# Causal scores in 64-token blocks with block-diagonal keys, in a gated linear-attention and ternary-FFN layer

## The reference

```python
Q, K, V = x @ Wq.T, x @ Wk.T, x @ Wv.T           # (B, L, H, 16) each
g = sigmoid(x . gw);  log_c = clip(cumsum(log g), -30, 30)
Gc = exp(log_c) + 1e-6;  R = silu(K . sw)
S = cumsum(K V^T * R / Gc, axis=1) * Gc           # a 16 x 16 state for every token
attn = (Q S) @ Wo.T
h = bitlinear(x, w_fc) + gate * (x @ v.T @ fast_b.T @ u.T)
ffn = bitlinear(relu(h) ** 2, w_proj)
out = x + attn + ffn                              # inside attn and ffn, x is normalised
```

## Time and profile before

| | us |
|---|---|
| median of 3 runs | 637.83 (637.13 to 639.09) |
| span of the profiled execution | 637.8 |
| PE busy | 620.1 (97%) |
| PEld busy | 545.8 (86%) |
| DVE busy | 528.7 (83%) |
| ACT busy | 443.3 (70%) |
| POOL busy | 387.3 (61%) |

### The profile page before, as it was taken

One profiled execution on the slowest core, in us unless ns is written; L12 is line 12 of the kernel. 1 busy time (PEld: TensorE's weight loads), 2 busy tenths in 40 slices (PEclk: granted clock), 3 DMA queues, 4 the chain that ended last, 5 costly groups with the idle time before them and its releaser, 6 DMA issues.

```text
span 637.8 us, 21397 instructions
## 1 busy us (share of the span) xinstructions
PE 620.1 (97%) x7710; PEld 545.8 (86%) x7710; DVE 528.7 (83%) x1241; ACT 443.3 (70%) x1036; POOL 387.3 (61%) x505
## 2 busy tenths in 40 slices
PE   7789999999999999999999999999999999999997
PEld 7667888888888888888888888888888888888886
DVE  7678978899888888898789988798988887897863
ACT  4568766677776667776666767775777766677664
POOL 4896666555656665556566565655565665666454
PEclk7689999999999999999999999999999999999999
DMA  9446656886796887866788887668887477775631
GB/s 303 104 97 107 131 106 147 136 145 131 139 147 109 141 138 130 143 133 128 121 145 132 132 146 145 125 106 136 134 143 151 117 137 131 135 130 124 115 54 51
DMA packets 190361, 83.31 MB, mean 131 GB/s; under 512 B 121888, under 2 KB 189728, under 8 KB 190256
## 3 DMA queue, kind: packets, MB, share of 16 engines
q1 hardware_dynamic: 188016, 79.32, 68.4%
q10 hardware_dynamic: 2240, 2.62, 1.3%
HBM read 12.43 MB, written 8.39 MB: 33 GB/s over the span
## 4 chain that ended last, share of the span: by engine, by line
PE 89%; POOL 4%; issue 2%; DMA 2%; SPq 1%; DVE 1%; ACT 1%; ACTq 0%; DVEq 0%; POOLq 0%
PE y_bank L2447 17%; PE attn_bank L2384 9%; PE hid_b L2418 8%; PE hid_a L2418 8%; PE front_b L2313 7%; PE y_bank L2462 7%; PE front_b L2272 7%; PE front_a L2294 6%; PE attn_bank L2397 4%; PE score_a L2346 4%; PE score_b L2346 4%; PE hid_b L2420 2%; PE hid_a L2420 2%; PE score_b L2361 2%; POOL sq_l L821 1%
## 5 line engine op out<-in xcount | busy, mean ns | idle before, releaser
L1871 DVE TENSOR_TENSOR sq_l<-relu_sq,sq_h 128x512 f16<-128x512 f32 x128 | 115.8, 907 | 3.7 <-ACT relu_sq L1162 2.6
L2447 PE MATMUL y_bank<-wproj_t,sq_h 128*128 128x256 f16 x504 | 117.0, 273 | 0.2 <-DVE sq_l L1871 0.2
L2447 PE MATMUL y_bank<-wproj_t,sq_l 128*128 128x256 f16 x504 | 117.0, 273 | 0.0
L1829 DVE TENSOR_TENSOR masked<-score_a,shapes_sb 128x512 f32<-128x512 f32 x128 | 88.2, 689 | 29.6 <-PE score_a L2346 29.0
L1829 DVE TENSOR_TENSOR masked<-score_b,shapes_sb 128x512 f32<-128x512 f32 x128 | 87.5, 684 | 14.0 <-PE score_b L2346 13.7
L746 POOL TENSOR_TENSOR state_diag<-state,state_mask 128x256 f32<-128x256 f32 x56 | 46.8, 836 | 70.7 <-DVE state L1847 34.3
L1153 ACT ACTIVATE sq_h<-relu_sq 128x512 f16<-128x512 f32 x128 | 79.0, 618 | 0.9
L1162 ACT ACTIVATE relu_sq<-relu_sq 128x512 f32<-128x512 f32 x128 | 78.7, 616 | 0.8 <-DVE sq_l L1871 0.7
L2418 PE MATMUL hid_b<-xt,wfc_t 128*128 128x256 f16 x512 | 73.6, 273 | 0.0
L2418 PE MATMUL hid_a<-xt,wfc_t 128*128 128x256 f16 x512 | 73.4, 273 | 0.1
L672 POOL TENSOR_SCALAR xn<-x_sb,neg_mean,rstd 128x256 f32<-128x256 f32 x64 | 42.3, 662 | 50.1 <-DVE rstd L1723 49.9
(11 more groups left out here) (224 smaller groups left out, 1656.9 us busy)
## 6 DMA issues: line engine op xcount, KB each, us to landing
q_diag<-q SPq DMA_DIRECT2D x256, 64.0 KB, 2.8
k_stack<-k SPq DMA_DIRECT2D x128, 128.0 KB, 4.3
x_sb<-in_x SPq DMA_DIRECT2D x32, 256.0 KB, 3.2
out_y<-y_both SPq DMA_DIRECT2D x31, 256.0 KB, 3.2
relu_sq<-in_w_fc ACTq DMA_DIRECT2D x1, 1024.0 KB, 11.5
pj_nat<-in_w_proj ACTq DMA_DIRECT2D x1, 1024.0 KB, 14.2
y_both<-in_w_qk ACTq DMA_DIRECT2D x1, 512.0 KB, 5.1
w_stage<-in_w_qkvz_t SPq DMA_DIRECT2D x1, 512.0 KB, 6.7
```

The lines of the kernel that those rows point to most:

```text
L1829: nc.vector.tensor_tensor(masked[:, c, g].rearrange("p (h n) -> p h n", h=4), score_bank[g % 2][:].rearrange("p (h n) -> p h n", h=4), cau ...
L1871: nc.vector.tensor_tensor(sq_l[:, q], sq[:, n], sq_h[:, q], ALU.subtract).then_inc(sq_l_done, 1)
L2447: last = mm(out_part(b, u, c), part[:, q, at:at + P], wproj_t[:, 2 * q + i], start=(q == i == n == 0 and (c == 0 or last_of_all(b, u))), s ...
```

## The change

- **Scores.** A chunk has `WAVES` = 3 waves. The stationary is now the 64 keys of both heads of a pair side by side (128 columns, block-diagonal in `k_diag`), and the moving operand is `q_stack`, the queries without padding. Waves 0 and 1: 4 matmuls each with the first 64 keys against all 128 queries. Wave 2: 8 matmuls with the later 64 keys against the later 64 queries. The block of later keys against earlier queries, which the mask made zero, is no longer computed.
- **Mask.** 6 a unit instead of 8, each still 512 columns, with a triangle for two heads (`causal_two`).
- **Values.** A chunk still has 16 column-tiled matmuls, but 8 move 128 columns and 8 move 64. The stationary is `v_pair`: rows 0 to 63 one head, rows 64 to 127 the other, so one matmul sums over both heads.
- **v_pair and v_all.** POOL writes the plain product `v_all` (for `state_updates`) in two steps, and in two more (`keep_rows`, 64 partitions x 256) the halves of `v_pair` that stay in their rows; DVE writes the other halves in two steps (`move_rows`, 64 partitions x 256, into the other 64 partitions).
- **DMAs of a unit.** `turn_keys` 2 transposes of 64 partitions instead of 1 of 128; `stack_keys` 8 of 128 KB instead of 4; `stack_queries` 4 of 128 KB instead of 8 of 64 KB.
- **Order.** All slots, prologues and epilogues are written anew. x is loaded and normalised one unit earlier, `queries_t` runs one unit earlier. In the prologue ACT does `fc_sums` ahead of the first `rstd_guess`, POOL `fc_highs(0)` ahead of the first `normalise`.

The diff, cut to its core; the new order of PE's slot is given whole:

```diff
-Q_DMAS, K_DMAS = 2 * PART, PART
+Q_DMAS, K_DMAS = PART, 2 * PART
+SUB = P // 2
+WAVES = 3
+ROW = CH * KT * 2 * P
...
             def stack_queries(b, u):
...
+                for n, part in enumerate((0, 1, 0, 1)):
+                    sp.dma_start(q_stack[32 * n:32 * n + 32, par], q16[:, part]).then_inc(q_stacked[par], 16)
...
             def turn_keys(b, u):
...
+                for h in range(2):
+                    sp.dma_start(k16[:].rearrange("p s (x h) z n -> p (s x) h z n", h=2)[:, :, h, 0],
+                                 k_tok16[SUB * h:SUB * h + SUB].rearrange("p s c d -> p (s c d)"),
+                                 transpose=True).then_inc(k_turned[u % 2], 16)
...
             def stack_keys(b, u):
...
+                for s in range(2):
+                    to = k_diag[:, par, SUB * s:SUB * s + PAIRS // KT * ROW].rearrange("p (g n) -> p g n", n=ROW)
+                    for n, part in enumerate((0, 0, 1, 1)):
+                        sp.dma_start(to[32 * n + HD * s:32 * n + HD * (s + 1)],
+                                     k16[64 * s:64 * s + 64, part]).then_inc(k_stacked[par], 16)
...
+            def keep_rows(b, u):
...
+                for s in range(2):
+                    rows = slice(SUB * s, SUB * s + SUB)
+                    nc.gpsimd.tensor_tensor(block_of(par, rows, s, s), heads_of(vg[:, par, :, 0:D], rows, s),
+                                            weights_of(par, rows, s), ALU.mult).then_inc(v_kept_done, 1)
...
+            def move_rows(b, u, s):
...
+                nc.vector.tensor_tensor(block_of(par, to, s, 1 - s), heads_of(vg[:, par, :, 0:D], rows, 1 - s),
+                                        weights_of(par, rows, 1 - s), ALU.mult).then_inc(v_moved_done, 1)
...
             def scores(b, u, c, g):
...
+                to = score_bank[(WAVES * c + g) % 2]
+                if g < KT:
+                    for i in range(PAIRS // KT):
+                        last = mm(to[:, i * P:(i + 1) * P], keys_of(par, i, c, g, 0),
+                                  q_stack[:, par, KT * i + g, c * P:(c + 1) * P], start=True, stop=True)
+                else:
+                    for t in range(KT):
+                        for i in range(PAIRS // KT):
+                            at = (t * (PAIRS // KT) + i) * SUB
+                            last = mm(to[:, at:at + SUB], keys_of(par, i, c, t, 1),
+                                      q_stack[:, par, KT * i + t, c * P + SUB:(c + 1) * P], start=True, stop=True)
...
             def values(b, u, c):
...
+                    for later in range(2):
                         for q in range(4):
...
+                            if later:
+                                cols = (4 * half + q) * SUB
+                                place, moving = slice(at + SUB, at + P), masked[:, c, KT, cols:cols + SUB]
+                            else:
+                                place, moving = slice(at, at + P), masked[:, c, half, q * P:q * P + P]
+                            last = mm(attn_bank[32 * q:32 * q + 32, place], v_pair[:, par, c, later, 4 * half + q], moving,
+                                      start=(c == half == later == 0), stop=False, skip_group_check=True)
...
             def slot(b, u):
                 values(*nxt, 0)
+                hidden(b, u, 3)
+                carried(*nxt, 0)
                 state_updates(*nxt)
+                cumulate(*after)
                 values(*nxt, 1)
+                keys(*unit_after(b, u, 3))
+                carried(*nxt, 1)
+                hidden(*nxt, 0)
                 projected(b, u, 0)
+                projected(b, u, 1)
                 scores(*after, 0, 0)
                 scores(*after, 0, 1)
                 values_gates(*unit_after(b, u, 3), 0)
                 scores(*after, 0, 2)
+                projected(b, u, 2)
+                hidden(*nxt, 1)
+                values_gates(*unit_after(b, u, 3), 1)
+                projected(b, u, 3)
+                scores(*after, 1, 0)
+                scores(*after, 1, 1)
+                queries_t(*unit_after(b, u, 4))
+                attn_projected(b, u)
+                hidden(*nxt, 2)
                 scores(*after, 1, 2)
```

More of the change, by code:

```diff
@@ L2011, in prologue @@
-                sums_taken(0, 1)
-                projection_scale()
-                mask(0, 1, 0, 0)
-                carry_state(0, 0, 1)
-                squares_low(0, 0, 1)
-                queries_low(0, 2)
-                mask(0, 1, 0, 1)
-                clip_log(0, 1)
-                refine_rstd(1, 0)
-                mask(0, 1, 0, 2)
-                mask(0, 1, 0, 3)
-                mask(0, 1, 1, 0)
-                mask(0, 1, 1, 1)
-                keys_low(0, 2)
-                mask(0, 1, 1, 2)
@@ L2026, in prologue @@
-                write_factors(0, 1)
-                unit_out(0, 0)
-                mask(0, 1, 1, 3)
-                z_low(0, 2)
+                clear_even_values()
+                stats_of(1, 1)
+                queries_low(0, 1)
+                scalars_of(1, 0)
+                clip_log(0, 0)
+                write_factors(0, 0)
+                rank_low(1)
+                keys_low(0, 1)
+                dens(0, 1)
+                refine_rstd(0, 3)
+                mask(0, 0, 0, 0)
+                log_low(0, 1)
@@ new lines, in prologue @@
+                scalars_of(1, 1)
+                carry_state(0, 0, 0)
+                clip_log(0, 1)
+                carry_state(0, 0, 1)
+                projection_scale()
+                write_factors(0, 1)
+                queries_low(0, 2)
+                output_inverse()
+                mask(0, 1, 0, 0)
+                keys_low(0, 2)
+                move_rows(0, 1, 0)
+                mask(0, 1, 0, 1)
+                move_rows(0, 1, 1)
+                mask(0, 1, 0, 2)
+                z_low(0, 2)
@@ L2059, in prologue @@
-                refine_rstd(1, 1)
-                z_low(0, 3)
-                carry_state(0, 2, 0)
-                sums_taken(0, 3)
-                scale_y(0, 0)
-                squares_low(0, 1, 3)
-                queries_low(1, 0)
-                carry_state(0, 2, 1)
-                mask(0, 3, 0, 0)
-                mask(0, 3, 0, 1)
-                keys_low(1, 0)
-                mask(0, 3, 0, 2)
-                mask(0, 3, 0, 3)
-                clip_log(0, 3)
-                mask(0, 3, 1, 0)
@@ L2080, in prologue @@
                 moments_of(1, 2)
+                sums_taken(0, 3)
+                squares_low(0, 1, 2)
+                carry_state(0, 2, 0)
+                scalars_of(1, 2)
+                squares_low(0, 1, 3)
+                z_low(0, 3)
+                carry_state(0, 2, 1)
+                refine_rstd(1, 2)
+                keys_low(1, 0)
+                clip_log(0, 3)
+                queries_low(1, 0)
+                unit_out(0, 2)
+                mask(0, 3, 0, 0)
+                write_factors(0, 3)
@@ L2596, in prologue @@
+                projected(0, 1, 3)
                 scores(0, 3, 0, 0)
@@ L2610, in prologue @@
-                scores(0, 3, 1, 3)
+                values(0, 3, 0)
                 hidden(0, 3, 0)
-                attn_projected(0, 1)
-                hidden(0, 3, 1)
-                values(0, 3, 0)
+                carried(0, 3, 0)
                 state_updates(0, 3)
+                projected(0, 2, 0)
                 values(0, 3, 1)
                 cumulate(1, 0)
-                carried(0, 3, 0)
-                queries_t(1, 1)
                 carried(0, 3, 1)
+                keys(1, 1)
@@ L2651, in epilogue @@
-                hidden(7, 3, 2)
-                projected(7, 2, 3)
                 attn_projected(7, 2)
```

934 lines of the change are left out of this document (468 added, 466 removed).

## The result

The changed kernel takes 720.94 us (719.07 to 722.0, median of 4) against 638.46 us for the kernel before, measured beside it: a ratio of 1.1284, interval 1.1254 to 1.1313. The forecast was 626, range 615 to 641. It was wrong in sign and by 95 us.

What follows compares the result with a forecast made beforehand. PE's stream of matmuls, busy 97% of 637.8 us, was taken as the bound; 637.8 - 13.4 (scores) - 13.4 (values) + 12.2 (array-mode changes) + 2 (start) + 1 (small waits) = 626.2 us, range 615 to 641.

Steps and rivals of the forecast that it cites:

- The matmuls: On PE, scores and values were each to save 0.21 us a chunk, 13.4 us apiece over 64 chunks.
- The entry behind `carried`: PE going from `carried` into column-tiled matmuls, a pair not shown: 0.14 us kept, 0.03 or 0.25 possible.
- free switches: Rival: on PE, array-mode entries behind `carried` and `cumulate`, and exits into them, cost nothing; 612 to 620 us, chance 0.12.
- weight loads that bound: Rival: in wave 2 of PE's scores each weight load takes 55 ns, 14.1 us more, 640 us; chance 0.08.
- SP and the DMAs: SP's issues take 16.5 of about 18.25 us a slot, DMA share 0.93 by bytes; counted as nothing.
- queue full: Rival: SP or the DMAs bind, 16.5 plus 2.8 us of waits making a 19.3 us slot; 654 us, chance 0.07.
- SP's half of that rival: The part of queue full in which SP binds, with 16.5 us of issues plus 2.8 us of waits a slot.
- late hand-over: Rival: DVE's mask for scores(0,2) comes 0.5 to 1.3 us late every slot; 644 us at 0.8 late; chance 0.16.
- The start: In the prologue, moving `fc_sums` and `fc_highs(0)` ahead of the first normalise costs net +2 us, bounds -2 to +6.
- The conditions set in the prediction: Forecast is wrong if PE idles over 10 us in 100 to 580 us, or tiled steps enter for under 0.1.

Runs made afterwards that it cites:

- e14_sp_in_time_split: e13 with PE's unit in the order of the changed kernel, values and carried apart, except for the late score; 634.2 us.
- e13: e7_stats_late with the load of x and, at an earlier place, the store of y issued by ACT instead of SP; 628.02 us.
- e1_rows_step4: The changed kernel with key and query transfers writing every fourth partition instead of neighbouring ones, same bytes; 653.73 us.
- e7_stats_late: e6 with DVE's `stats_of`, which waits for x, moved behind one mask and one `squares_low`; 640.11 us.
- e4: e1_rows_step4 with the score that waits for the mask moved behind two other steps of PE; 650.50 us.
- e6: e1_rows_step4 with PE's column-tiled steps together, the waiting score later and the start ordered as before the change; 641.19 us.
- e2: The changed kernel with only the order of a unit's eight key transfers changed; 688.97 us.

## Why the prediction was wrong, point by point

**The matmuls were priced right.** In e14_sp_in_time_split PE is busy 467.78 of 470 us, as before the change, and its chain shows one term after another:

```profile
303.90 0.23 PE score_b L2441 x8
304.13 0.80 PE attn_bank L2485 x32
304.93 0.54 PE hid_b L2517 x4
...
306.57 0.58 PE score_b L2457 x32
307.16 0.14 PE front_a L2413
307.29 0.80 PE attn_bank L2485 x32
308.09 1.42 PE front_a L2381 x12
...
312.79 0.22 PE score_a L2435 x4
```

The wave of eight 64-column matmuls takes 0.23 us (0.22 taken, 0.44 the bound by slow weight loads). A values step takes 0.80 = 0.66 + 0.14 where it enters the column-tiled mode, 0.66 where it doesn't (307.45 in e13's chain). Behind an exit `hidden` takes 0.54 for 0.44, `cumulate` 0.14 for 0.03, and `keys` 1.42, as `queries_t` did before. The entry behind `carried` costs 0.13 here and 0.18 in e1_rows_step4, where I had kept 0.14. So both rivals about the matmuls, free switches and weight loads that bound, fall. The middle units of e14 take 18.10 against 18.50 before: 0.40 saved, with 0.42 forecast (18.67 to 18.25).

**The step that failed is "SP and the DMAs", counted as nothing.** I took the DMA share by bytes, 0.76 to 0.93, at the price of a byte before. The bytes weren't the trouble: with other rows (e1) the same bytes take 0.67, less than the 0.76 before. The price was: written to 16 neighbouring partitions at 204 GB/s they took 0.99, and 67 us of the 82 were this. The rival "queue full" had the right place and 7 in 100; but its price, 654, counted SP's issues alone and had no term for where a transfer writes. That the earlier trace rows gives eight transfers in 5.16 us, and the diff doubles their size with their number and 16 rows unchanged, would have led there: 0.5 MB to 1 MB through the same rows in the same time.

**SP's half of that rival was real too.** I summed 16.5 us of issues a unit and left 1.7 for waits. They took 17.4 in a stretch of e7_stats_late, as single issues last 1.9 to 2.5 us, and SP bound at 18.35 a unit; without that the unit is 17.85. With the groups split, 18.57 in e1, against 18.10 in e14. What makes single issues long was not tried.

**The late hand-over was real in its mild form.** The wait for the mask, 9.5 us in 22 places in e1, is the one that I had fitting by 0.15 us. From the end of the state to the mask DVE's list took 6.4 us there (303.92 to 310.35), where I had summed 5.4. It was hidden under the DMAs in the changed kernel (40.7 us in 20 places, led by x), and came out when they were mended. Asking for the score later gained 3.2 us at most (e4), and then SP stood behind it.

**The start was mis-sized.** +2 us, bounds -2 to +6, was forecast, with the first `values` 4 to 5 us later; it is 14.2 us later, and undoing the new start gives 8.7 us, with the first `values` 6.0 us earlier; why it is still 5.4 us later than before wasn't tried. I had held the start's chain to be POOL's comparisons, and so let the late normalisation of unit 0 hide beside them. But the comparisons themselves ended 7.7 us later (at 54.5 us, 46.8 before, 47.8 in e6).

**What no term of mine held** is that the first three units take 60.7 us in e14 and 52.6 before, with the old start and all else mended. The first y is 6.5 us earlier in turn. Together this is 1.6 us more than before, and the last three units with the end are 1.2 us more. So six of the 30 units gain nothing, and e14's span is 631.0, not 637.8 - 30 x 0.40 = 625.8. Why these units don't gain was not tried.

**Together.** 721 = 626 forecast, + 67 for the rows written (e1), + 7 for the start (8.7 where 2 was forecast), + 21. Of these 21, 11 went with SP's relief and the later score (653.7 - 634.2, less the start's 8.7); 10 are still there in e14, the first and last units among them. The parts were measured one upon another and need not add up in another order.

**The conditions set in the prediction.** PE's idle from 100 to 580 us was to be under 10 us; it was 46. The entry was to cost at least 0.1; it cost 0.13 to 0.18.

## What to carry to other kernels

Price a transfer by the partitions that it writes, not by its bytes alone: where a change doubles the size of transfers into a few neighbouring partitions, divide the size by the time between two issues and look whether transfers of that shape already land later than larger ones. Sum the queue's issue time for each unit as you sum an engine's, and take a sum that comes close to the unit for a bound: here 16.5 us were summed for a unit of 18.25, and three more issues cost their full length. And before a transfer changes its queue or its place, name who waits for it: with one store issued some 4 us later the kernel lost 82 us, and moving it ahead again gave back 60, five times what relieving its queue brought.

## What the runs showed of the hardware that was not expected

The same 128 KB landed in 5.8 us on 16 neighbouring partitions and in 2.4 us on every fourth of 64, in an otherwise equal kernel, and the price fell on all others in the queue: x landed in 7.4 us, and in 4.1. Ordering the same 16-row transfers so that none is followed at once by the one 32 partitions further on gave half of it back (e2). SP's issue of a plain transfer took about 0.6 us at 64, 128 and 256 KB alike, and a single transpose's issue up to 4.83 us while the DMA engines were full.
